# Four small PSUM items moved from the ring of two double banks to the ring of two single banks, with a new order of all steps

## The reference, cut to what matters

```python
x = layernorm(x + L0_attn(x))        # gated recurrence with ternary weights, and a gated FFN
x = layernorm(x + L0_xattn(x, ctx))  # attention with 16 heads of 16 channels, rotary positions
x = layernorm(x + L0_ffn(x))         # weights of +1 and -1: 512 -> 1024 -> 1024 -> 256, relu

# the part that the change touches
scores = einsum('bhqd,bhkd->bhqk', Q, K) * SCALE
attn = softmax(scores)               # needs the largest score of each row
out = einsum('bhqk,bhkd->bhqd', attn, V)
x2 = layernorm(x1 + out @ Wo.T + bo)
```

## Time and profile before

| | |
|---|---|
| median of 3 runs | 849.92 us (847.07 to 851.01) |
| profiled execution | 846.09 us, of which the span of the trace is 844.2 us |
| PE busy | 786.2 us (93% of the span) |
| DVE, ACT, POOL busy | 611.8, 579.5, 317.9 us |
| mean granted TensorE clock | 0.979 of 2.4 GHz |

### The profile page before, as it was taken

One profiled execution on the slowest core, in us unless ns is written; L12 is line 12 of the kernel. 1 busy time (PEld: TensorE's weight loads), 2 busy tenths in 40 slices (PEclk: granted clock), 3 DMA queues, 4 the chain that ended last, 5 costly groups with the idle time before them and its releaser, 6 DMA issues.

```text
span 844.2 us, 18112 instructions
## 1 busy us (share of the span) xinstructions
PE 786.2 (93%) x6893; PEld 572.9 (68%) x6926; DVE 611.8 (72%) x1199; ACT 579.5 (69%) x960; POOL 317.9 (38%) x562
## 2 busy tenths in 40 slices
PE   1897768999999999999999999999999999999996
PEld 1454326677786868686867768686868777776675
DVE  5754768696978788786969687878879696857242
ACT  6665476959687786869595967778695959563622
POOL 6983225251433423453424343342434251330010
PEclk9999589999999999999999999999999999999998
DMA  9003010203020211111020302111120202020000
GB/s 306 8 26 107 13 33 4 87 2 90 14 82 22 61 42 43 61 37 55 16 86 14 89 14 71 33 58 45 39 64 15 77 14 64 14 64 14 2 13 26
DMA packets 53029, 40.69 MB, mean 48 GB/s; under 512 B 7344, under 2 KB 52432, under 8 KB 52944
## 3 DMA queue, kind: packets, MB, share of 16 engines
q1 hardware_dynamic: 52944, 39.53, 15.5%
HBM read 26.66 MB, written 12.59 MB: 46 GB/s over the span
## 4 chain that ended last, share of the span: by engine, by line
PE 84%; DVE 8%; ACT 4%; issue 2%; POOL 1%; ACTq 0%; DVEq 0%; POOLq 0%
PE bankC L1321 27%; PE bankA L1258 7%; PE bankA L1172 7%; PE bankC L1305 6%; PE bankC L1337 6%; PE bankA L1107 5%; PE slotB L1245 4%; PE slotB L1227 4%; PE slotB L1179 3%; PE bankA L1088 3%; PE bankA L1179 3%; DVE nmax L1625 2%; PE bankC L1353 2%; PE slotB L1277 2%; PE bankA L1098 2%
## 5 line engine op out<-in xcount | busy, mean ns | idle before, releaser
L1321 PE MATMUL bankC<-h0h,w 128*128 128x256 f16 x1024 | 232.4, 273 | 0.5 <-DVE h0l L1669 0.5
L1321 PE MATMUL bankC<-h0l,w 128*128 128x256 f16 x1024 | 231.8, 273 | 0.0
L1625 DVE TENSOR_REDUCE nmax<-slotB 128x4 f32<-128x1024 f32 x128 | 153.9, 1215 | 17.5 <-PE slotB L1227 17.5
L964 ACT ACTIVATE pr<-slotB,cscale 128x1024 f32<-128x1024 f32 x128 | 139.1, 1118 | 10.9 <-PE slotB L1245 10.6
L1321 PEld LDWEIGHTS bankC<-h0h,w 128*128 128x128 f16 x1024 | 100.2, 98 | 28.6 <-issue 14.1
L1321 PEld LDWEIGHTS bankC<-h0l,w 128*128 128x128 f16 x1024 | 100.2, 98 | 15.4
L1258 PE MATMUL bankA<-pr,v_aug 128*32 128x256 f32 x1024 | 69.5, 389 | 0.0
L1669 DVE SCALAR_TENSOR_TENSOR h1l<-bankC,h1h 128x512 f16<-128x512 f32 x64 | 43.5, 679 | 25.8 <-ACT h1h L994 25.6
L1305 PE MATMUL bankC<-xh,w 128*128 128x256 f16 x256 | 58.6, 273 | 1.9 <-DVE h0l L1669 1.1
L745 POOL TENSOR_TENSOR qt<-qb,turn 128x256 f32<-128x256 f32 x32 | 22.7, 730 | 98.8 <-ACT qb L918 98.8
L1337 PE MATMUL bankC<-w,h1h 128*128 128x256 f16 x256 | 59.1, 273 | 0.7 <-DVE h1l L1669 0.6
(11 more groups left out here) (253 smaller groups left out, 1779.0 us busy)
## 6 DMA issues: line engine op xcount, KB each, us to landing
x<-in_x SPq DMA_DIRECT2D x16, 256.0 KB, 2.9
cT<-in_ctxT SPq DMA_DIRECT2D x16, 256.0 KB, 3.0
scr<-kpart SPq DMA_DIRECT2D x16, 256.0 KB, 2.6
k_st<-scr SPq DMA_DIRECT2D x32, 128.0 KB
scr<-qpart SPq DMA_DIRECT2D x16, 256.0 KB, 2.3
q_st<-scr SPq DMA_DIRECT2D x32, 128.0 KB, 2.7
out<-x SPq DMA_DIRECT2D x16, 256.0 KB, 2.1
k_st<-scr SPq DMA_DIRECT2D x32, 64.0 KB
```

The costliest lines, as they stand in the source:

```text
L964: act.activation(pr[i % 2][:, c, :, :].rearrange("p h s -> p (h s)"), slotB[ringB.slot(g, name)][:, :], ACT.Exp, scale=cscale[:, g:g + 1])\
L1321: ins = pe.matmul(bankC[ringC.slot(g, name)][:, e * T:(e + 1) * T], w_1[:, i // 2, (2 * m + e) * P:(2 * m + e + 1) * P], (h0h, h0l)[i % 2] ...
L1625: dve.tensor_reduce(nmax[:, 0:H * NT].rearrange("p (a q b n) -> p q n a b", a=2, q=NHG, b=2)[:, hg, n], slotB[ringB.slot(g, name)][:, :].r ...
```

## The change

Four items of each group move from ring B to ring A: `max` (the turned maxima), `oT` (turned outputs), `wo` (output projection) and `x2T` (turned second residual). Ring A then has 23 items for each group instead of 19 and ring B 17 instead of 21. PE, ACT and DVE do the same instructions as before on `bankA` instead of `slotB`. The helper `across` is replaced by `transposed`, which issues the same transposes. ACT's square of the context (`cn`) waits in addition for its own predecessor of group g - 1, since both write the same scratch. And both tables are replaced by others, so that the order on every engine and all slots change.

```diff
-           "pv0": ("ACT", "pv1"), "pv2": ("ACT", "pv3")}
-B_ITEMS = {**{f"score{u}": ("DVE", f"score{u}") for u in range(NT * NHG)}, "max": ("DVE", "max"),
+           "oT": ("ACT", "oT"), "wo": ("DVE", "wo"), "x2T": ("DVE", "x2T"), "max": ("DVE", "max"), "pv0": ("ACT", "pv1"), "pv2": ("ACT", "pv3")}
+B_ITEMS = {**{f"score{u}": ("DVE", f"score{u}") for u in range(NT * NHG)},
            **{f"exp{i}.{c}": ("ACT", f"exp{i}.{c}") for i in range(NHG) for c in range(NT)},
-           "oTok": ("DVE", "oTok"), "oT": ("ACT", "oT"), "wo": ("DVE", "wo"), "x2T": ("DVE", "x2T")}
+           "oTok": ("DVE", "oTok")}
...
             def maxrow(g):
-                sp.wait_ge(*ringB.emptied(g, "max"))
+                sp.wait_ge(*ringA.emptied(g, "max"))
...
+                if g >= 1:
+                    act.wait_ge(*csq_s.at(g - 1))
                 act.activation(junk[:, 2].rearrange("p n d -> p (n d)"), flat(cT[g % 2]), ACT.Square,
...
             def wo_(g):
-                pe.wait_ge(*ringB.emptied(g, "oT"))
+                pe.wait_ge(*ringA.emptied(g, "oT"))
-                take(g, ringB, "wo")
-                across_tokens(slotB[ringB.slot(g, "wo")], oT, w_o).then_inc(ringB.full_sem(g, "wo"), 1)
+                take(g, ringA, "wo")
+                across_tokens(bankA[ringA.slot(g, "wo")], oT, w_o).then_inc(ringA.full_sem(g, "wo"), 1)
```

More of the change, by code:

```diff
@@ L69 @@
     "weights": """
[L70 to L74, removed]
@@ L81 @@
-        w:tab V34.438 | w:wk G40.558 | w:wq G47.854""",
-    "recurrent": """
[L83 to L88, removed]
+        w:s V-277.36 P-28.252 | w:m V-250.072 A-30.271 P-23.763 | w:a V-100.503 | w:iv V-38.234
@@ new lines @@
+        w:h27 P40.809 | w:h28 P74.717 | w:h29 P37.68 | w:h30 P36.776 | w:h31 P71.836
+        w:mask V33.406 S32.131 P35.119 | w:sgn V13.558 | w:k0 V41.085 | w:k2 V37.632 | w:k1.0 A31.839
+        w:k1.1 A34.229 | w:k1.2 A66.206 | w:k1.3 A79.631 | w:rope G12.376 P14.901 A18.111
+        w:bqk P17.822 A23.504 | w:sq A18.406 P20.764 V27.956 G30.064 | w:bs G37.055 A61.199
+        w:tab V37.892 | w:wk G20.206 | w:wq G32.225""",
+    "recurrent": """
+        loadx S28.594 | scale A6.907 G7.365 V-1.093 | stat1 G17.341 | round V12.278
+        xqT P14.332 A16.962 | iv0 P18.752 A21.32 V22.572 | iv1 P23.933 A25.684 V24.513
+        a P17.323 A19.424 | aT P22.127 A24.473 | sq A26.731 | ivT P27.351 V32.021 | cum V33.495
+        recur V33.759 | rec P33.376 A36.651 V35.536 | max2 V35.768 | stat2 G43.315 | round2 V37.529
+        rqT P37.943 A42.364 | gate0 P40.405 A44.994 V48.065 | gate1 P43.874 A46.617 V48.126
+        stat3 G56.157 | round3 V48.281 | sqT P51.16 A54.078 | down P54.478 V56.344 | bn V57.875 G70.843
+        x1 V62.763""",
@@ L96 @@
-        qput S48.232 | qget S59.123""",
+        x1T P62.746 A65.577 | xb G76.158 | q P65.61 A68.316 | rotq G78.405 V69.603 | qp A72.652 V76.268
+        qput S50.178 | qget S50.659""",
     "scores": """
-        score0 P87.979 V93.15 | score1 P90.322 V93.309 | score2 P91.195 V95.365 | score3 P92.451 V98.336
-        score4 P97.504 V100.697 | score5 P100.358 V101.528 | score6 P104.779 V106.732
-        score7 P104.847 V109.45 | max P111.522 A112.037 V113.346 | maxrow S74.319""",
+        score0 P88.948 V91.872 | score1 P90.966 V93.219 | score2 P91.288 V94.071
@@ L101 @@
+        score3 P93.011 V98.949 | score4 P99.76 V102.122 | score5 P100.467 V103.839
+        score6 P104.486 V107.589 | score7 P104.959 V110.182 | max P112.222 A113.307 V114.003
+        maxrow S84.902""",
     "values": """
-        exp0.0 P117.255 A120.536 | exp0.1 P117.385 A120.849 | pv0 P121.816 | exp1.0 P120.362 A122.954
-        exp1.1 P120.73 A123.069 | pv1 P123.601 A127.325 | exp2.0 P122.237 A123.138
-        exp2.1 P122.244 A125.74 | pv2 P124.015 | exp3.0 P123.662 A125.995 | exp3.1 P123.794 A127.435
@@ L105 @@
-        pv3 P128.552 A133.387 | oTok P130.85 V136.093 | oT P135.548 A137.529 | wo P138.997 V140.577
-        bn2 V141.116 G149.518 | x2 V145.874""",
-    "network": """
[L108 to L115, removed]
+        exp0.0 P116.962 A119.242 | exp0.1 P117.74 A120.411 | pv0 P121.137 | exp1.0 P120.97 A120.866
@@ L946, in max_high @@
                     act.wait_ge(*max_in.at(g - 1))
-                act.wait_ge(*ringB.filled(g, "max"))
-                act.activation(m_hi[:, :], slotB[ringB.slot(g, "max")][0:NT * H, 0:P], ACT.Copy, scale=1.0 / K_HIGH)\
+                act.wait_ge(*ringA.filled(g, "max"))
+                act.activation(m_hi[:, :], bankA[ringA.slot(g, "max")][0:NT * H, 0:P], ACT.Copy, scale=1.0 / K_HIGH)\
                    .then_inc(mhi_s.sem, 1)
@@ L986, in x2_high @@
                     act.wait_ge(*ringC.filled(g - 1, f"l0_{KT // 2 - 1}"))
-                act.wait_ge(*ringB.filled(g, "x2T"))
-                act.activation(flat(xh), slotB[ringB.slot(g, "x2T")][:, 0:512], ACT.Copy).then_inc(xh_s.sem, 1)
+                act.wait_ge(*ringA.filled(g, "x2T"))
+                act.activation(flat(xh), bankA[ringA.slot(g, "x2T")][:, :], ACT.Copy).then_inc(xh_s.sem, 1)
             def layer_high(g, item, m, dst, done, later):
@@ L1234, in max_ @@
                     pe.wait_ge(*ringB.emptied(g, f"score{un}"))
-                take(g, ringB, "max")
-                pe.transpose(slotB[ringB.slot(g, "max")][:, 0:P], nmax[:, :], ident[:, :])\
-                  .then_inc(ringB.full_sem(g, "max"), 1)
+                take(g, ringA, "max")
+                pe.transpose(bankA[ringA.slot(g, "max")][:, 0:P], nmax[:, :], ident[:, :])\
+                  .then_inc(ringA.full_sem(g, "max"), 1)
             def shifted(g, i, c):
@@ L1632, in max_low @@
                 dve.wait_ge(*mhi_s.at(g))
[L1633 to L1634 removed]
+                dve.scalar_tensor_tensor(m_lo[:, :], m_hi[:, :], -K_HIGH, bankA[ringA.slot(g, "max")][0:NT * H, 0:P],
+                                         ALU.mult, ALU.add).then_inc(ringA.free_sem(g, "max"), 1)
             def divided(g):
```

94 lines of the change are left out of this document (48 added, 46 removed).

## The result

| | before | after |
|---|---|---|
| median of 7 runs each | 849.92 us (847.07 to 851.16) | 846.78 us (845.96 to 848.65) |
| ratio, 95% interval | | 0.9967 (0.9951 to 0.9982) |
| the same on another chip, 22 and 12 runs | 848.61 us (845.53 to 853.02) | 847.37 us (845.76 to 848.79) |
| ratio there | | 0.9986 (0.9969 to 1.0003) |
| profiled execution, its span | 846.09, 844.2 us | 847.72, 845.9 us |

Forecast were 851.0 us and, most likely, no change of more than 0.5%. The time lies inside the range and within 0.5%, but it went the other way: 3.1 us down, and 1.2 on the other chip, where the interval just reaches 1. Worse, the small sum hides two large terms that nearly cancel, and neither was forecast at its size.

What follows compares the result with a forecast made beforehand. PE was taken to bound the steady stretch, chains through several engines the ends. Steady +0.4, head +0.9 and tail -0.2 gave +1.1 us on the 849.9 us median: 851.0 us, range 844.0 to 856.5 (8 in 10).

Steps and rivals of the forecast that it cites:

- PE alone sets the pace and 4.4 us are all that any order could win back: Steady stretch, 148 to 778 us: PE busy for 625.57 of 630 us, so at most 4.4 us to gain.
- Each run of half-height matmuls that starts or stops: PE's borders of small-matmul runs: about 0.1 us each, 318 before and 320 after, so 0.
- Exponentials' new places, +0.4: Two more places a group where PE may wait for ACT's exponential: 0 to 3.9 us, taken as 0.4.
- The moved items, 0: Four items moved to ring A: PE time unchanged and no new waits, 0; other end 4.2 us.
- the rival's price: Ring A: `v` or `x2T` waits for DVE, 0.3 us in each of 14 groups; 857 us in all, chance 12%.
- Head, +0.9: Start of the run, groups 0 to 2: queue and order changes on several engines sum to 0.9 us slower.
- The POOL step: Group 0: `w_q` ahead on POOL delays `cg(0)` to 48.1 and `gate0(0)` to about 50.0; taken as 2.2 us.
- slower, by POOL's queue: Group 0: long `w_k` and `w_q` put `gate0(0)` at 52.1, idle work at half rate follows; 855.5 us, chance 14%.
- clock case: Head, 98 to 119 us: PE kept fed regains full clock, some 4.2 us; 844.2 us in all, chance 22%.
- the second filler (+0.9): Group 0 on PE: idle work in front of `gate1` doubles, 0.9 us slower.
- DVE's order (-1.0): Head: DVE takes `x2(0)` and the second residual's low part earlier, so `l0_0(0)` comes 1.0 us sooner.
- The forecast's own sign: End of the head: the forecast counts as right if `l0_0(0)` starts within 1.5 us of 141.7.

Runs made afterwards that it cites:

- e9: Changed kernel with two stretches of small matmuls in the exponentials split by parts of the second layer: 854.66 us, 1.0076 of the kernel before.
- e3: Kernel before with its own order on all engines, only the four items moved to ring A: 872.70 us, 1.0290 of the kernel before.
- e6: Kernel before, unchanged, profiled once more: profiled execution 847.2 us, median of its runs 848.6 us.
- e7: Changed kernel, unchanged, profiled and timed once more beside the kernel before: 847.37 us, ratio 0.9986.
- e8: Changed kernel with POOL's queue in the head as before, PE's order kept: 843.63 us, 0.9940 of the kernel before.
- e11: Changed kernel with POOL's head queue as before and two idle weight products around group 0's second gate product moved later: 843.78 us, 0.9944 of before.
- e4: Kernel before, rings untouched, with `score4` moved next to `score5` and both parts of `exp2` directly behind `pv0`: 869.96 us, 1.0242 of before.

## Why the prediction was off, by its own steps

- **"PE alone sets the pace and 4.4 us are all that any order could win back": false, and the first step that failed.** Busy time is no floor. It includes what borders cost, 229 at 0.10 us in twelve groups or 1.9 us a group, and waits of up to 0.2 us, and an order can win that back without changing the busy share. The row that seemed to confirm the step, 2.1 us over 13 short waits, shows missing records. That the gain of the thirteen groups, 4.1 us, stayed below 4.4 is chance.
- **"Each run of half-height matmuls that starts or stops costs PE about 0.1 us, but there are 318 such borders before and 320 after: 0": the price was right, the count wrong.** It took the products for full matmuls. A stretch into which products are drawn (`exp1.0 pv0 exp1.1 exp2.0`) has one start and one stop; counted so, 303 borders that cost became 273. At 0.1 us this is -3.0 in the whole run and -2.5 in the twelve groups. The term was 0. e9 shows the price from the other side. The rest of the groups' gain, about 2 us, has terms that the forecast didn't have: `wo` away from the scores and `cn` (-1.1) and short waits (-0.9).
- **Exponentials' new places, +0.4: -0.4 net.** No wait of PE on ACT's exponentials is recorded in the steady stretch, but from start to start they cost 4.2 us in the twelve groups before and 3.8 after. The new places do cost something, as the forecast had it (`exp2.0` 1.4 us, `score0` 1.1 more); it missed that the old order paid at its own (`exp1.1` 1.8 us, gone, and `exp3.1` 1.9, now 0.8).
- **The moved items, 0: right for this order.** The tight place was named rightly, `v` behind `down`; e3 shows what it costs in another order, 1.3 us a group, four times the rival's price.
- **Head, +0.9: +3.1 (e6 to e7) to +5.9.** The POOL step had the right chain and the right end, `cg(0)` and `gate0(0)` within 0.3 us; in between luck helped: `stat2(0)` ran from 41.73 to 45.91 instead of 42.6 to 46.7, and the context steps behind it took 1.95 us instead of 1.4. Its price was wrong: 2.2 us against a `gate0(0)` at 47.26, but that row was itself late. PE's keys' projection ahead of it, in that execution (granted clock 0.51 from 41 to 44.5 us) and in e6 (1.00):

```profile
40.84 3.56 PE L1172 MATMUL bankA<-cT,w_k 128*128 128x256 f32 x8 [2.13 <-issue]
40.68 1.97 PE L1172 MATMUL bankA<-cT,w_k 128*128 128x256 f32 x8 [1.58 <-issue]
```

  In e6 `gate0(0)` starts at 45.4, and with POOL's old queue at 45.2 to 45.5. Against that it is 4.2 us at the gate, and e8 gives 3.7 us of the median back. Behind the gate the idle work ran at half clock, which the forecast had only in its rival "slower, by POOL's queue" and only for a `gate0(0)` from about 51 on; it came at 49.6. The pause ahead of the gate that the forecast counted against its clock case, about 4 us, is there (4.46), and its price is here and not around 100 us. e11, where that work runs at full clock, shows 0 for the second filler (+0.9); for the changed kernel itself, where the two take 3.62 us, it wasn't tried. `exp1.1` behind `pv0` (+0.7) shows nothing: `exp0.0` to `oTok` takes 17.1 and 17.0 us before, 16.8 in both executions after. DVE's order (-1.0): `wo(0)` to `l0_0(0)` takes 9.5 us in both executions before; with the new order it takes 8.3 to 8.5 in six executions and 9.8 to 10.0 in three, so the gain of 1 us came in six of nine. `cn(1)` and `xqT(1)` were not tried alone. The forecast's own sign, `l0_0(0)` within 1.5 us of 141.7, failed: 147.6 and 146.2.
- **Tail, -0.2: 0.** 102.7 us in both.
- **SP's queue and the added wait, 0: nothing seen** against it.
- **The rival "faster, by the clock" was wrong too.** The granted clock is 0.73 and 0.67 in 80 to 100 and 100 to 120 us after, against 0.64 and 0.68: no full clock there. The kernel became faster by a mechanism that the forecast had put at zero, and by two that it didn't have.

Sum as found: head +3.1 to +5.9, groups -4.1, tail 0. That is -1.0 to +1.8, and the medians say -1.2 and -3.1. The rest is on the side of before: its two profiled executions, 846.1 and 847.2 us, lie below its medians of 848.6 to 849.9, those of the changed kernel don't lie below its own by more than 1.1. In e3 and e4, which have the old head queues, `score0(0)` starts at 88.1 and 88.5 instead of 85.2 and 87.2, with a granted clock of 0.83 from 60 to 80 us. So late heads of 1 to 3 us occur in the old order; whether they fill the gap stays open, since no trace of a slower run of the kernel before was taken.

## What to carry to other kernels

Count PE's cost from start to start of its pieces, not from busy time, and count every border between full and small matmuls, products with few columns included: gather small pieces into few stretches. Compare the start of a piece with the end of the engine that frees its bank; a wait of 0.1 us may not be drawn. And where a wait has no releaser, look whether all matmuls of that instruction are in the trace. An order and the rings under it are one thing; half a change of the two cost 1.3% and 2.9% here. Price a head from two profiles at least: the row that carried the largest term was 1.9 us off its usual place.

## What the hardware showed

- Full to small, small to full and score to product cost 0.10 us each at full clock, the way out of a product 0.01.
- A shifted score that waits for ACT to free its slot starts 0.055 us behind the end of ACT's exponential, a score that stands behind a product 0.144 us behind it (24 and 12 places in either kernel).
- Steady groups repeat within 0.02 us from execution to execution (599.73 and 599.61 in thirteen); the head doesn't, by 1.3 to 2.0 us between two of the same kernel.
- Of POOL's scalings those were long that ran beside one DVE instruction, a conversion of 2,048 uint8 to half precision. Before it ran at 37.78 us beside the first of `w_k` (1.94 us, the second 1.07); after, at 38.87 us beside the first of `w_q` (2.05, the second 1.07), while `w_k` in its new place, beside a DVE instruction on `xg`, took 1.08 and 1.11. For that place the prediction had estimated both long, 3.9 us, from the Trainium skill, GPSIMD Engine Reference, section Key points. The trace has 2.15.
